# Attention's third score chunk moved ahead of the slot projection into the projection banks, with ScalarE's chunk copies placed between the halves of the value squares

## The reference

```
q, k, v, s, g = x @ Wq, x @ Wk, x @ Wv, clip(x @ Ws), x @ Wg      # per head, DK = M = 64, DV = 128
z  = cumlogsumexp(s) over time
ok = q . sum over earlier t' of k[t'] p[t']   (running state, decayed)  # slot scores, causal
pv = softmax(ok)
o  = pv . sum over earlier t' of p[t'] v[t']                            # causal again
o  = o * rsqrt(mean(o^2) + eps) * g_norm_weight * silu(g)
x  = layernorm(x + o @ Wo)
```

## Time and profile before

| what | before |
|---|---|
| median of three executions | 2053.84 us |
| the profiled execution | 2056.06 us, span 2054.1 us |
| TensorE busy | 1997.3 us, 97% of the span |
| TensorE weight loads | 1435.8 us, 70% |
| VectorE | 1386.9 us, 68% |
| ScalarE | 770.8 us, 38% |
| GpSimd | 526.1 us, 26% |
| attention's 32 steps | about 38 to 1225 us of the span |
| one middle step | 37.1 us |

### The profile page before, as it was taken

The page is one execution under the profiler, slowest core; times in us unless marked ns, Lnnn a source line. Parts: engine busy times, 40 slices in busy tenths (PEclk is TensorE's granted clock), DMA queues, the critical chain, the costliest instruction groups (busy, mean ns, idle before and its releaser), DMA issues. The chain is left out here.

```text
span 2054.1 us, 30669 instructions
## 1 busy us (share of the span) xinstructions
PE 1997.3 (97%) x11828; PEld 1435.8 (70%) x11828; DVE 1386.9 (68%) x2234; ACT 770.8 (38%) x1903; POOL 526.1 (26%) x575
## 2 busy tenths in 40 slices
PE   7999999999999999999999988999999999999997
PEld 6787877877878778777787854444434378787875
DVE  4666666666566666666666678999999655555556
ACT  3333232232322323223223324888888721212111
POOL 2132142151141242243143253222221011111111
PEclk9999999999999999999999998999999999999999
DMA  4000100100001001001000000111110100000002
GB/s 164 1 1 11 37 1 11 37 10 20 19 11 36 1 11 36 1 11 37 1 11 4 6 12 16 26 26 30 26 25 21 31 16 16 31 15 31 16 16 82
DMA packets 58608, 46.88 MB, mean 23 GB/s; under 512 B 14448, under 2 KB 47216, under 8 KB 58480
## 3 DMA queue, kind: packets, MB, share of 16 engines
q1 hardware_dynamic: 58480, 45.11, 7.3%
HBM read 32.78 MB, written 4.19 MB: 18 GB/s over the span
## 5 line engine op out<-in xcount | busy, mean ns | idle before, releaser
L1606 DVE TENSOR_REDUCE a_raw_qks<-a_ps 128x1 f32<-128x512 f32 x512 | 321.9, 683 | 20.1 <-PE a_ps L871 18.7
L1536 ACT ACTIVATE x_prob<-a_ps 128x512 f32<-128x512 f32 x512 | 279.0, 606 | 71.2 <-PE a_ps L893 70.2
L66 PE MATMUL a_ps<-a_vg_hi,a_xT_lo 128*128 128x512 f32 x512 | 209.6, 409 | 0.8 <-DVE a_vg_lo L1631 0.8
L67 PE MATMUL a_ps<-a_vg_lo,a_xT_hi 128*128 128x512 f32 x512 | 200.4, 391 | 0.0
L68 PE MATMUL a_ps<-a_vg_hi,a_xT_hi 128*128 128x512 f32 x512 | 199.9, 390 | 0.0
L66 PE MATMUL a_ps<-a_xT_hi,a_qks_lo 128*128 128x512 f32 x384 | 157.9, 411 | 1.9 <-DVE a_xT_lo L1637 1.9
L1658 DVE SCALAR_TENSOR_TENSOR a_gate<-a_gate,a_ps 128x256 f32<-128x256 f32 x128 | 51.9, 406 | 152.1 <-ACT a_gate L1427 152.1
L871 PE MATMUL a_ps<-a_xT_lo,a_xT_hi 64*128 64x512 f32 x384 | 146.1, 465 | 6.6 <-DVE a_raw_qks L1606 4.9
L68 PE MATMUL a_ps<-a_xT_hi,a_qks_hi 128*128 128x512 f32 x384 | 150.9, 393 | 0.0
L67 PE MATMUL a_ps<-a_xT_lo,a_qks_hi 128*128 128x512 f32 x384 | 150.6, 392 | 0.0
L723 POOL TENSOR_TENSOR a_f<-a_rs 128x8 f32<-128x8 f32 x32 | 6.5, 202 | 560.5 <-ACT a_flat L1455 560.5
(11 more groups left out here) (190 smaller groups left out, 4572.9 us busy)
## 6 DMA issues: line engine op xcount, KB each, us to landing
a_raw_vg<-in_L_attn_Wv_dram SPq DMA_DIRECT2D x8, 512.0 KB, 4.3
a_raw_vg<-in_L_attn_Wg_dram SPq DMA_DIRECT2D x8, 512.0 KB, 6.2
a_raw_qks<-in_L_attn_Wo_dram SPq DMA_DIRECT2D x8, 512.0 KB, 3.7
a_xT_lo<-a_xT_lo SPq DMA_DIRECT2D x32, 128.0 KB, 2.4
out_dram<-acc SPq DMA_DIRECT2D x8, 512.0 KB, 3.2
x_values<-acc SPq DMA_DIRECT2D x13, 256.0 KB, 2.8
acc<-in_x_dram SPq DMA_DIRECT2D x3, 1024.0 KB, 9.5
f_raw_down<-in_L_ffn_down_w_dram SPq DMA_DIRECT2D x11, 256.0 KB, 2.9
```

Source lines behind the costliest of these rows:

```text
L66: pe.matmul(out, w_lo, x_hi, start=start, stop=False)
L67: pe.matmul(out, w_hi, x_lo, start=False, stop=False)
L1536: nc.scalar.activation(prob[par][:, s % 4, :], score_bank(q, s, par), ACT.Exp, scale=X_SCALE).then_inc(exp_done[par], 1)
L1606: nc.vector.tensor_reduce(nm[:, q % 2, i % 4, par, i // 4:i // 4 + 1], max_bank(u, q, i, par), AX.X, ALU.max, negate=True).then_inc(max_re ...
```

## The change

- `last_chunk` comes ahead of `next_project(S)`, so the three chunks stand together and S and VG behind them. In steps 0 to 30 it writes the two projection banks pj (`last_chunk_banks`) and has no wait of its own; step 31 keeps ch and the waits.
- For m >= 1 the S projection goes to ch[0] (`slot_bank`) and waits for ScalarE's copy of the first chunk (`chunk_act`). VG and VG+1 wait for VectorE's masks of the third chunk (`chunk_dve`), which free the pj banks.
- ScalarE's order is: four squares (ob[0]), copy of the first chunk, four squares (ob[1]), copy of the second chunk.
- GpSimd's `factor(n - 1)` stands behind `mask_diagonals(n)`, no longer at the end of step n-1.
- VectorE's order is the same; the banks that `clip` and the masks of the third chunk read are others.

```
--- before.py
+++ after.py
@@ -334,6 +334,14 @@
         EARLY = 6
         IN_VALUES = 10
 
+        def slot_bank(m, b):
+
+            return ch[0] if m else pj[b % 2]
+
+        def last_chunk_banks(n):
+
+            return ch if n == NSTEP - 1 else [pj[n % 2], pj[(n + 1) % 2]]
+
         def value_banks(n):
 
             return (okb, tb) if n == NSTEP - 1 else ob
@@ -742,6 +750,7 @@
                 last_pair = at(p, PAIRS - 1)
                 mask_diagonals(n)
                 if not first:
+                    factor(n - 1)
                     scale_o(n)
                 if n == NSTEP - 2:
                     clear_queries(0)
@@ -763,8 +772,6 @@
                     pool.wait_ge(proj_done, PROJ * (n + 1) + Q)
                     split_s(p + 1)
                     split_vg(p + 1)
-                if n < NSTEP - 2:
-                    factor(n)
 
             def last_step(n):
                 mask_diagonals(n)
@@ -937,16 +944,20 @@
 
             def project(m, i, b, pair):
 
-                bank = pj[(b + i) % 2]
+                bank = slot_bank(m, b) if i == S else pj[(b + i) % 2]
 
                 if i == S:
-                    wait(pe, right_ready, 2 * m - 1)
+                    wait(pe, chunk_act, 2 * m - 1)
                     pe.wait_ge(s_ready, pair + 1)
                 elif i == VG:
-                    wait(pe, left_ready, 2 * m - 1)
+                    if m:
+                        pe.wait_ge(chunk_dve, 4 * m - 1)
                     pe.wait_ge(vg_ready, pair + 1)
                 elif i == VG + 1:
-                    pe.wait_ge(clip_done, m + 1)
+                    if m:
+                        pe.wait_ge(chunk_dve, 4 * m)
+                    else:
+                        pe.wait_ge(clip_done, 1)
                 else:
                     pe.wait_ge(gate_ready, 4 * m + i - 2)
                 if i == Q:
@@ -986,10 +997,11 @@
 
             def last_chunk(n):
 
-                pe.wait_ge(chunk_act, 2 * n + 1)
-                pe.wait_ge(chunk_dve, 4 * n + 1)
+                if n == NSTEP - 1:
+                    pe.wait_ge(chunk_act, 2 * n + 1)
+                    pe.wait_ge(chunk_dve, 4 * n + 1)
                 for i, col, first in CHUNKS[2]:
-                    mm = blocks(ch, i, col, first, T)
+                    mm = blocks(last_chunk_banks(n), i, col, first, T)
                 mm.then_inc(chunk_done, 1)
 
             def diagonals(n):
@@ -1071,9 +1083,8 @@
                 pe.wait_ge(e_ready, n + 1)
                 into = n == NSTEP - 2
                 chunks(n)
-                next_project(S)
                 last_chunk(n)
-                next_project(VG)
+                next_project(S, VG)
                 slots(n)
                 states(n, j)
                 if not first:
@@ -1427,9 +1438,11 @@
                     nc.scalar.activation(gate[:, b % 2, i - VG, :], bank[:, 2 * DV:4 * DV], ACT.Tanh,
                                          scale=0.5).then_inc(tanh_ready, 1)
 
-            def copy_chunks(n):
+            def copy_chunks(n, squares_of=None):
                 act.wait_ge(chunk_done, 3 * n + 1)
                 nc.scalar.copy(causal[:, 0, 0:T], ch[0]).then_inc(chunk_act, 1)
+                if squares_of is not None:
+                    square_sums(squares_of, 1)
                 act.wait_ge(chunk_done, 3 * n + 2)
                 nc.scalar.copy(causal[:, 0, CHUNK_AT[1]:CHUNK_AT[1] + T], okb).then_inc(chunk_act, 1)
 
@@ -1444,17 +1457,17 @@
                 act.wait_ge(e_done, m + 1)
                 nc.scalar.copy(e[:, :, :].rearrange("p i c -> p (i c)"), tb).then_inc(e_ready, 1)
 
-            def square_sums(n):
+            def square_sums(n, half):
                 ob = value_banks(n)
-                act.wait_ge(o_done, n + 1)
-                for half in range(2):
-                    if half:
-                        act.wait_ge(og_ready, 2 * n + 1)
-                    for t in range(TT):
-                        g = 2 * t + half
-                        sq = nc.scalar.activation(squares[:, g, 0:DV], ob[half][:, t * P:(t + 1) * P], ACT.Square,
-                                                  scale=DV ** -0.5, accum_out=ss[:, g:g + 1])
-                    sq.then_inc(sq_done, 1)
+                if half:
+                    act.wait_ge(og_ready, 2 * n + 1)
+                else:
+                    act.wait_ge(o_done, n + 1)
+                for t in range(TT):
+                    g = 2 * t + half
+                    sq = nc.scalar.activation(squares[:, g, 0:DV], ob[half][:, t * P:(t + 1) * P], ACT.Square,
+                                              scale=DV ** -0.5, accum_out=ss[:, g:g + 1])
+                sq.then_inc(sq_done, 1)
 
             def step(n, p, j, first):
                 b1 = (j + 1) % B
@@ -1463,7 +1476,7 @@
                     for i in groups:
                         copy_proj(n + 1, i, b1)
 
-                copy_chunks(n)
+                copy_chunks(n, None if first else n - 1)
                 act.wait_ge(chunk_done, 3 * n + 3)
                 high_left(eT[:, :])
                 into = n == NSTEP - 2
@@ -1491,10 +1504,10 @@
                 act.wait_ge(diag_done, n + 1)
                 next_proj(Q, K)
                 copy_e(n + 1)
-                square_sums(n)
+                square_sums(n, 0)
 
             def last_step(n):
-                copy_chunks(n)
+                copy_chunks(n, n - 1)
                 act.wait_ge(chunk_done, 3 * n + 3)
                 high_left(eT[:, :])
                 act.wait_ge(sub_ready, n + 1)
@@ -1502,7 +1515,8 @@
                 copy_oT(n)
                 act.wait_ge(wT_ready, n + 1)
                 high_right(wT)
-                square_sums(n)
+                square_sums(n, 0)
+                square_sums(n, 1)
                 copy_keys(1, 1)
                 for i in range(1, TILES):
                     copy_queries(1, 1, i)
@@ -1650,7 +1664,7 @@
 
             def clip(m, b):
                 dve.wait_ge(proj_done, PROJ * m + 1)
-                nc.vector.tensor_scalar(eT[:, :], pj[b % 2], CLAMP, -CLAMP, ALU.min, ALU.max).then_inc(clip_done, 1)
+                nc.vector.tensor_scalar(eT[:, :], slot_bank(m, b), CLAMP, -CLAMP, ALU.min, ALU.max).then_inc(clip_done, 1)
 
             def gating(m, i, b):
 
@@ -1755,7 +1769,7 @@
                 norm_now = at(p, PAIRS - 1) and j > 0
                 into = n == NSTEP - 2
                 mask_chunks(n, ((0, 1, ch[1]), (1, 1, tb)))
-                mask_chunks(n, ((2, 0, ch[0]), (2, 1, ch[1])))
+                mask_chunks(n, ((2, 0, last_chunk_banks(n)[0]), (2, 1, last_chunk_banks(n)[1])))
                 low_left(eT[:, :], 2 * n + 1)
                 dve.wait_ge(left_ready, 2 * n + 2)
                 clip(n + 1, b1)
```

45 lines of the change are left out of this document (27 added, 18 removed).

## The result

The kernel after takes 2039.04 us (median of four runs, 2037.68 to 2041.06); the kernel before took 2054.30 us beside it (2053.28 to 2054.87). The ratio is 0.9924, interval 0.9911 to 0.9938: 15.3 us, or 0.76%, faster. The forecast was 2040.5 us from a gain of 13.3 us. The interval of the ratio is a gain of 12.7 to 18.3 us, so the forecast gain lies inside it, and the times alone can't say whether it was too small; the traces can, in part. Attention's steps came out as written. A gain behind them was not in the forecast, and where it came from takes up most of what follows.

What follows compares the result with a forecast made beforehand. TensorE's instruction stream was taken as the bound, busy 37.11 of 37.12 us in a step. 0.43 us less in each of 31 steps is 13.3 us, so 2053.84 - 13.3 = 2040.5 us; range of 8 in 10, 2038.8 to 2045.0.

Steps and rivals of the forecast that it cites:

- Two of three changes of shape go: TensorE, steps 0 to 30: only the chunks-to-S change stays; 6.29 us for 6.72, 0.43 us less a step.
- S to VG costs nothing: TensorE, from S's last product to VG: same shape, so the usual distance of 0.23 us.
- Rival 1: TensorE, S to VG: as dear as a change of shape, leaving 0.23 us a step, 7.1 us, 2046.7; 3 in 100.
- S's wait: S on TensorE waits for ScalarE's copy of the first chunk: margin 0.07 us, cost taken as nothing, bounds 0 to 3 us.
- Rivals 2 and 3: S's copy wait: 2, copy partly late, 2044.5 to 2047.6, 8 in 100; 3, late beyond the gain, slower, 5 in 100.
- VG, the slots and `out_rows` have their cover: Waits for masks and the scaled output cost nothing: cover 0.8 us for VG, 3.2 for the slots, 1.1 for scaled output.
- Rival 4: Later in the step, VectorE or GpSimd chains give the gain back: within 0.2% of now; 5 in 100.
- In step 31 ... I count nothing there: Step 31: first chunk's copy ends a microsecond sooner, but the slots wait for VectorE's masks (0.3 us); no gain counted.
- the wait on two semaphores goes: Third chunk on TensorE: needs no wait now; the old one ended long before in any case.
- No DMA moves: The step's new waits: no DMA is moved by the change, and SP's waits are on the splits; no size given.

Runs made afterwards that it cites:

- five squares: Kernel after with one more square of ob[1] ahead of the first chunk's copy on ScalarE: 2043.06 us, ratio 0.9943.
- all eight: Kernel after with ScalarE's old order, both copies behind the eight squares: 2065.94 us in one run.
- 112: Kernel before with 225 satisfied waits more on TensorE's queue ahead of the first projection, which added 112 instructions: 2057.88 us.

## Why the prediction was right, and where it was wrong

- **Two of three changes of shape go, 0.43 us a step.** The sum's parts, measured in step 16 in the order of the prediction: 0.18 for 0.17; 0.23 for 0.23; 0.23 for 0.21; S 2.66 for 2.61; 0.22 for 0.23; VG's first distance 0.23; the rest to the slots 2.59 for 2.61. From 626.62 to the slots at 632.96 it is 6.34 us, where the prediction had 6.29 and the kernel before 6.72. That is 0.38 in this step and 0.41 in the mean of steps 1 to 29; the mean is inside the bounds of 0.40 to 0.46. The 0.05 us missing in S stand in its first distances, some of 0.24 where 0.23 was usual. S takes 2.66 us in 21 of the 31 steps and 2.61 in the ten others. I found no cause for it.
- **S to VG costs nothing.** Rival 1 is out: 0.22 us, with another stationary operand and a wait. By the rule of the Trainium skill's "TensorE: Matmul & The Clock Gate", Part 3, it should have cost time; the row doesn't bear that out. What did cost was the change between the chunks' shape and the projections', in two places of the program. (In rival 1, the 0.23 us a step and the 7.1 us are the gain that would be left, 0.43 less 0.20.)
- **S's wait is covered, by 0.12 us for 0.07.** Rivals 2 and 3 had the right place and the right price: five squares gave 0.13 us a step, all eight 0.88.
- **VG, the slots and `out_rows` have their cover**: 1.0, 3.5 and 1.35 us, for 0.8, 3.2 and 1.1. `scale_o` took 1.90 us with VectorE busy for 0.53 of them, where it had taken 2.35 with VectorE busy for 2.32; that the one makes the other was not tested. Rival 4 is out.
- **"In step 31 ... I count nothing there": this is the step that failed**, with all that lies behind it. 31 x 0.43 = 13.3 against 12.7 measured is a miss of 0.6 us the other way; some 2.6 us of gain (15.3 less 12.7, as near as the medians tell) lay in a part that the sum left out, because the change touches no work there. It does touch the number of instructions ahead of it: the prediction says "the wait on two semaphores goes" and prices that at nothing, and it says "No DMA moves". Both hold within the step and not for the program behind it, where 31 instructions fewer move the fetches out of two loads of keys that TensorE waits for. That is shown and worth 1.1 to 1.8 us; the rest of the 2.6 is open. The range's low end had 0.7 us for all this (2038.8 for 2039.5). From the trace of before the gap could have been found, as a wait of 1.92 us for `keys_in_place` with a packet of instructions inside the load; that it would go could not, since a shift by 31 instructions could as well have moved another fetch onto a load, as it did with 112 (a gap of 1.65 us at 380).

## What to carry to other kernels

Where TensorE's stream is the bound, look at the distances between starts, not at durations: every change between pairs on 64 rows of the array and products on 128 cost here some 0.1 us before and 0.05 to 0.1 behind, and the gain of grouping is only had if the banks let the groups stand together and every engine that must free a bank does so first. When an order is changed, the work behind the first wait to come must be counted out to the single operation (here one square, 0.25 us, decided). And a change that adds or takes instructions in a long unrolled program can move the time elsewhere by a few microseconds, so a forecast's range needs room for it, and a verdict on a gain of that size needs the parts measured apart.

## What the runs showed of the hardware that I had not expected

- A fetch of 16 KB of TensorE's instructions that fell into a load held back the load's last four packets until it ended, so the load landed 1.0 to 1.7 us late, and TensorE, which waited for it, was idle for 0.4 to 1.1 us (eleven times in six profiles). Where nothing waited for the data, it cost nothing that shows.
- The idle time of a TensorE row can be put down to "issue" where TensorE waited for a DMA on a semaphore: 0.93 us here, inside a wait of 1.92.
- A wait that is satisfied is not free on TensorE: 450 of them took 19.6 us of the time ahead of step 0, 225 took 6.4 (78.36 for 71.96 us at step 1), and 62 nothing, in a place where TensorE was idle for 1.9 us anyway.
- A row that names one releaser for a wait on two semaphores can name the one that was long done: the copy had ended 0.96 us before.
